# A gated cross-attention and feed-forward kernel: the weighing of values as three fp32r products over the whole array instead of four fp32 column tiles

## The reference

```
q = layernorm(x) @ Wq            # 32 heads of 32
k, v = ctx @ Wk, ctx @ Wv        # 8 key-value heads of 32, each serves 4 query heads
scores = q k^T / sqrt(32)
attn = softmax(scores)
out = attn v                     # per head: 128 queries x 128 keys, by 128 keys x 32
x = x + tanh(g_xattn) * (out @ Wo)
x = x + tanh(g_ffn) * ffn(layernorm(x))
```

## Time and profile before

| | |
|---|---|
| median of 3 runs | 1945.35 us (1944.39 to 1946.03) |
| the profiled execution's own time | 1945.35 us |
| its span, first to last instruction | 1943.6 us |
| mean granted TensorE clock | 0.995 of full speed |
| busy: TensorE, VectorE, ScalarE, GpSimd | 98%, 60%, 45%, 44% of the span |
| matmul instructions of PV | 512, from 67.2 to 627.5 us |

### The profile page before, as it was taken

How to read it: one execution, slowest core, us unless ns; L and a number is a source line. 1 busy time by engine, 2 the same in 40 slices (tenths; PEclk the granted TensorE clock), 3 DMA queues, 4 the chain that set the end, 5 groups by cost and what they waited for, 6 DMA issues and landing times.

```text
span 1943.6 us, 27413 instructions
## 1 busy us (share of the span) xinstructions
PE 1903.7 (98%) x9312; PEld 1555.2 (80%) x9312; DVE 1171.9 (60%) x1622; ACT 884.2 (45%) x2109; POOL 848.1 (44%) x632
## 2 busy tenths in 40 slices
PE   7999999999999999999999999999999999999999
PEld 6768877877876888888888878888888888887887
DVE  7657656755764865555555567765555555545565
ACT  4883793596387343333332344443333333333333
POOL 1330341232133588888888411114675766630000
PEclk9999999999999999999999999999999999999999
DMA  5225226324424235354545866662232333257665
GB/s 207 85 96 198 88 61 219 125 61 167 150 63 182 94 125 200 135 183 156 179 153 183 282 221 237 211 222 98 91 125 81 108 108 108 87 189 249 214 222 186
DMA packets 125948, 298.78 MB, mean 154 GB/s; under 512 B 12704, under 2 KB 21920, under 8 KB 120480
## 3 DMA queue, kind: packets, MB, share of 16 engines
q1 hardware_dynamic: 125568, 297.06, 44.8%
q10 hardware_dynamic: 288, 0.52, 0.1%
HBM read 221.25 MB, written 71.57 MB: 151 GB/s over the span
## 4 chain that ended last, share of the span: by engine, by line
PE 79%; ACT 10%; DVE 3%; DMA 3%; issue 2%; POOL 2%; SPq 0%; POOLq 0%; ACTq 0%; DVEq 0%
PE ps L1593 25%; PE ps L1595 25%; PE ps L1594 25%; ACT pb L918 6%; ACT pt L861 1%; DMA xo<-x1d 1%; PE ps L1653 1%; DMA raw<-ws 1%; ACT qo_l L861 1%; PE ps L1643 1%; PE ps L1689 1%; DVE qo_l L1203 1%; DVE qo_h L1203 1%; PE ps L1809 1%; ACT qo_h L861 1%
## 5 line engine op out<-in xcount | busy, mean ns | idle before, releaser
L1593 PE MATMUL ps<-xop_h,w_h 128*128 128x512 f32 x1208 | 471.8, 391 | 0.0
L1595 PE MATMUL ps<-xop_h,w_l 128*128 128x512 f32 x1208 | 470.1, 389 | 0.0
L1594 PE MATMUL ps<-xop_l,w_h 128*128 128x512 f32 x1208 | 469.9, 389 | 0.0
L1171 DVE TENSOR_TENSOR bl<-raw,bh 128x1024 fp32r<-128x1024 f32 x154 | 197.4, 1289 | 146.6 <-ACT bh L861 146.6
L861 ACT ACTIVATE bh<-raw 128x1024 fp32r<-128x1024 f32 x154 | 163.1, 1061 | 233.8 <-PE ps L1595 212.8
L1595 PEld LDWEIGHTS ps<-xop_h,w_l 128*128 128x128 f32 x1208 | 226.7, 188 | 47.1
L1593 PEld LDWEIGHTS ps<-xop_h,w_h 128*128 128x128 f32 x1208 | 226.8, 188 | 46.6 <-DVE cc L1405 0.3
L1594 PEld LDWEIGHTS ps<-xop_l,w_h 128*128 128x128 f32 x1208 | 226.8, 188 | 46.4
L1593 PE MATMUL ps<-bh 128*128 128x512 f32 x616 | 244.9, 398 | 6.0 <-DVE xo L1496 3.4
L1171 DVE TENSOR_TENSOR w_l<-fraw,w_h 128x512 fp32r<-128x512 f32 x130 | 135.9, 1046 | 185.8 <-ACT w_h L861 185.8
L1595 PE MATMUL ps<-bh,bl 128*128 128x512 f32 x616 | 241.6, 392 | 0.0
(11 more groups left out here) (156 smaller groups left out, 3447.9 us busy)
## 6 DMA issues: line engine op xcount, KB each, us to landing
fraw<-in_wf SPq DMA_DIRECT2D x42, 1024.0 KB, 5.1
raw<-hs SPq DMA_DIRECT2D x154, 256.0 KB, 3.0
hs<-hsum SPq DMA_DIRECT2D x22, 1280.0 KB, 5.7
raw<-ws SPq DMA_DIRECT2D x110, 256.0 KB, 3.9
wc_raw<-in_wc SPq DMA_DIRECT2D x44, 512.0 KB, 4.5
dw<-in_wd SPq DMA_DIRECT2D x11, 1024.0 KB, 7.7
hs<-hb SPq DMA_DIRECT2D x44, 256.0 KB, 2.0
raw<-in_wd SPq DMA_DIRECT2D x44, 256.0 KB, 3.9
```

The lines of the kernel that those rows point to most:

```text
L1171: return nc.vector.tensor_tensor(out, whole, hi.bitcast(F32), ALU.subtract)
L1593: pe.matmul(out, w_hi_, m_h, start=first, stop=False, skip_group_check=goes_on)
L1594: pe.matmul(out, w_hi_, m_l, start=False, stop=False, skip_group_check=goes_on)
L1595: return pe.matmul(out, w_lo_, m_h, start=False, stop=last, skip_group_check=goes_on)
```

## The change

`weigh_values` becomes twelve fp32r matmuls for each pair: `three` for each of the four heads, into the whole 128 partitions of bank 5, summed over the heads (the sum starts at the first head and ends at the last). The weights are 128x128 tiles `vp_h` and `vp_l`, zero but for the 32 columns of the head. For that:

- the transposed probabilities and the values are kept as high and low parts: ScalarE's copies write the high ones, and VectorE gets a subtraction for each unit (`pt_out`) and for each sequence's values (`v_out`);
- GpSimd clears `vp_h`, `vp_l` once a group and copies the values into their places, two copies for each pair (`build_vp`); there are two buffers, so the copies for pair m + 2 wait for PV of pair m (`pv_done`);
- waits for `pt_ready` and `v_ready` on TensorE become waits for the low parts, and PV waits for `vp_built` too.

```diff
-        pt = at("pt", [P, 2, 4, 2 * P], F32, o_x1)
+        pt_h = at("pt_h", [P, 2, 4, 2 * P], F32R, o_x1)
+        pt_l = at("pt_l", [P, 2, 4, 2 * P], F32R, o_x1 + 8192)
...
-        vc = at("vc", [P, NB, 2 * P], F32, o_vc)
+        vc_h = at("vc_h", [P, NB, 2 * P], F32R, o_vc)
+        vc_l = at("vc_l", [P, NB, 2 * P], F32R, o_vc + 4096)
...
+        vp_h = at("vp_h", [P, 2, 4, P], F32R, o_vp)
+        vp_l = at("vp_l", [P, 2, 4, P], F32R, o_vp + 4096)
...
+            def build_vp(m):
+
+                a, b = m // NB // 2, m % NB
+                for vp, vc in ((vp_h, vc_h), (vp_l, vc_l)):
+                    dst = bass.AP(vp, (m % 2) * 4 * P, [[8 * P, P], [P + HD, 4], [1, HD]])
+                    ins = nc.gpsimd.tensor_copy(dst, vc[:, b, a * P:(a + 1) * P].rearrange("p (j d) -> p j d", j=4).bitcast(F32))
+                ins.then_inc(vp_built, 1)
...
+                nc.gpsimd.memset(vp_h[:, :, :, :].bitcast(F32), 0.0)
+                nc.gpsimd.memset(vp_l[:, :, :, :].bitcast(F32), 0.0).then_inc(vp_zero, 1)
+                pool.wait_ge(vp_zero, g + 1)
+                pool.sem_inc(passed, 1)
+                pool.wait_ge(v_lo, g * NB + NB)
+                pool.sem_inc(passed, 1)
+                build_vp(0)
+                build_vp(1)
                 for n in range(UNITS):
...
                     nc.gpsimd.tensor_tensor(p, p, r, ALU.mult).then_inc(normed, 1)
+                    if n >= 5 and n % 2 == 1:
+                        m = (n - 5) // 2
+                        pool.wait_ge(pv_done, g * PAIRS + (m + 1))
+                        pool.sem_inc(passed, 1)
+                        build_vp(m + 2)
...
+            def v_out(G, b):
+                dve.wait_ge(v_hi, G * NB + (b + 1))
+                minus(vc_l[:, b, :], ps[:, b % 2, 2 * P:4 * P], vc_h[:, b, :]).then_inc(v_lo, 1)
...
+            def pt_out(g, n):
+                m, gi = n // 2, n % 2
+                dve.wait_ge(pt_hi, g * UNITS + (n + 1))
+                where = (slice(None), m % 2, slice(None), slice(gi * P, (gi + 1) * P))
+                minus(pt_l[where], ps[:, 3 + n % 2, :].rearrange("p (j q) -> p j q", j=4), pt_h[where]).then_inc(pt_lo, 1)
...
                         o_out(g, m)
+                    if 3 <= n < UNITS + 3:
+                        pt_out(g, n - 3)
...
             def weigh_values(g, m):
-                pe.wait_ge(pt_ready, g * UNITS + (2 * m + 2))
+                pe.wait_ge(pt_lo, g * UNITS + (2 * m + 2))
+                pe.wait_ge(vp_built, g * PAIRS + (m + 1))
                 if m >= 1:
                     pe.wait_ge(o_lo, g * PAIRS + m)
-                k, b = m // NB, m % NB
                 for j in range(4):
-                    head = slice(HD * j, HD * j + HD)
-                    ins = pe.matmul(ps[head, 5, 0:2 * P], vc[:, b, k // 2 * P + HD * j:k // 2 * P + HD * j + HD],
-                                    pt[:, m % 2, j, :], start=True, stop=True, tile_position=(0, HD * j))
+                    ins = three(ps[:, 5, 0:2 * P], vp_h[:, m % 2, j, :], vp_l[:, m % 2, j, :],
+                                pt_h[:, m % 2, j, :], pt_l[:, m % 2, j, :], j == 0, j == 3)
                 ins.then_inc(pv_done, 1)
```

More of the change, by code:

```diff
@@ L236, in gated_cross_attention_ffn @@
         q_hi, q_lo = sem("q_hi"), sem("q_lo")
-        pt_ready = sem("pt_ready")
+        pt_hi, pt_lo = sem("pt_hi"), sem("pt_lo")
         o_hi, o_lo = sem("o_hi"), sem("o_lo")
-        v_ready = sem("v_ready")
+        v_hi, v_lo = sem("v_hi"), sem("v_lo")
         k_hi, k_lo = sem("k_hi"), sem("k_lo")
@@ L255, in gated_cross_attention_ffn @@
         kb_zero = sem("kb_zero")
+        vp_zero = sem("vp_zero")
         kb_first = sem("kb_first")
         kb_in = [sem(f"kb_in{c}") for c in range(2)]
+        vp_built = sem("vp_built")
         maxed = sem("maxed")
@@ L886, in kv_out @@
                 copy(kn[:, b % 2, :], ps[:, b % 2, 0:2 * P]).then_inc(k_nat, 1)
-                copy(vc[:, b, :], ps[:, b % 2, 2 * P:4 * P]).then_inc(v_ready, 1)
+                copy(vc_h[:, b, :], ps[:, b % 2, 2 * P:4 * P]).then_inc(v_hi, 1)
             def kt_out(G, b):
@@ L909, in pt_out @@
                     act.wait_ge(pv_done, g * PAIRS + (m - 1))
-                copy(pt[:, m % 2, :, gi * P:(gi + 1) * P],
-                     ps[:, 3 + n % 2, :].rearrange("p (j q) -> p j q", j=4)).then_inc(pt_ready, 1)
+                copy(pt_h[:, m % 2, :, gi * P:(gi + 1) * P],
+                     ps[:, 3 + n % 2, :].rearrange("p (j q) -> p j q", j=4)).then_inc(pt_hi, 1)
             def exps(g, n):
@@ L1347, in body @@
                     normalise1(G, 3, next_x(3))
+                    v_out(G, 0)
                     split_ct(G, 2)
                     split_wc(G, 0)
+                    v_out(G, 1)
                     split_ct(G, 3)
@@ L1354, in body @@
                     split_wc(G, 1)
+                    v_out(G, 2)
                     k_out(G, 1)
@@ L1357, in body @@
                     xt_out(G, 3)
+                    v_out(G, 3)
                     k_out(G, 2)
@@ L1518, in _ @@
             normalise1(0, 0, x1[:, 0, :])
+            v_out(0, 0)
             normalise1(0, 1, x1[:, 1, :])
@@ L1524, in _ @@
             dve.wait_ge(tg_ready, 1)
+            v_out(0, 1)
             normalise1(0, 3, x1[:, 3, :])
@@ L1528, in _ @@
             xt_out(0, 0)
+            v_out(0, 2)
             k_out(0, 1)
@@ L1534, in _ @@
             split_wc(0, 1)
+            v_out(0, 3)
             k_out(0, 2)
@@ L1625, in scores @@
                 if n == 1:
-                    pe.wait_ge(v_ready, g * NB + NB)
+                    pe.wait_ge(v_lo, g * NB + NB)
                 elif n == 2:
@@ L1665, in kv @@
                 if b >= 2:
-                    pe.wait_ge(v_ready, G * NB + (b - 1))
+                    pe.wait_ge(v_lo, G * NB + (b - 1))
                 for k in ks:
@@ L1694, in body @@
                 pe.wait_ge(xt1_lo, g * 8 + 8)
-                pe.wait_ge(v_ready, g * NB + NB - 1)
+                pe.wait_ge(v_lo, g * NB + NB - 1)
                 q_tile(g, 0, range(K8))
```

2 lines of the change are left out of this document (1 added, 1 removed).

## The result

| | before | after |
|---|---|---|
| median | 1945.69 us (1944.39 to 1946.70, 4 runs) | 1975.36 us (1974.56 to 1978.11, 4 runs) |
| ratio to before, 95% interval | | 1.0155 [1.0138, 1.0173] |
| the profiled execution's own time | 1945.35 us | 1973.73 us |
| its span | 1943.6 us | 1971.4 us |
| mean granted TensorE clock | 0.995 | 0.999 |

The changed kernel is slower by 29.7 us; 1973.6 was predicted, in a range of 1962 to 1988.

The account below looks back on a forecast made before the run. TensorE, busy 98% of the span, was taken as the bound: 1945.35 + 40.7 for longer PVs - 12.4 of waits taken back = 1973.6 us. The forecast was 1967 to 1981 (chance 0.62), the 8-in-10 range 1962 to 1988.

Parts of the forecast that it names:

- The matmuls: TensorE's PV in the attention: twelve matmuls 0.117 us apart add 0.64 or 0.63 us each PV, 40.7 us gross.
- Rival D: PV's old form runs four passes a head one after the other, so the change wins 30 us: 1915 us; chance 0.02.
- What waits give back: TensorE's waits near PV and the transposes take back 3.1 us a group, 12.4 us for four.
- every other PV of the first stage: Odd PVs there lose their 0.30 us wait as TensorE's road gets longer: four a group, 1.2 us back.
- The PV in front of the long wait: Inside the 8.54 us chain from ninth to tenth PV, with its 2.34 us wait: one PV hidden, 0.63 us back.
- The end of the group: From unit 26's transposes to unit 31's, two PVs, 1.28 us, fit in 1.54 us of waits: 1.3 us back.
- VectorE at nothing: VectorE's 128 new subtractions, 87 us in all, add 0 us since row maxima stay in time; bound 22 us.
- GpSimd at nothing: GpSimd's 128 new casts, 0.4 us each, fit in its waits and add 0 us; bound 8 us.
- A: VectorE's subtraction or GpSimd's casts become a wait, nothing is taken back: 1996 us, half of it 1985; chance 0.19.
- B: ScalarE paces the attention loop more than seen, partly hiding TensorE's time; 27.9 us of waits go: 1958 us; chance 0.14.
- C: In steps with a PV, ScalarE sets the round throughout and PV runs in its shadow: 1945 us; chance 0.03.
- The place: TensorE's span grows only in the attention, about 7 us a group; first-stage four-unit round from 11.06 to about 12.0 us.

Follow-up runs that it names:

- the helpers alone: Changed kernel with its new VectorE and GpSimd work and waits, but PV again as four fp32 matmuls in column tiles, high parts only: 1950.22 us, 1.0027 to the kernel before.
- the moved copies: Kernel before, with the copies of transposed probabilities of the odd units from 9 to 31 of each group moved from ScalarE to VectorE: 1937.74 us, 0.9971.
- the order edit: Kernel before, with the query tile's split moved behind the split of the pair's output on ScalarE and VectorE: 1938.48 us, 0.9966.

## Why the prediction was right, point by point

*The matmuls: right.* Forecast 0.64 and 0.63 us a PV, measured 0.67 and 0.64: 10 x 0.67 + 6 x 0.64 = 10.5 us a group, 42 in all for 40.7. The score matmuls of the earlier trace rows were the right like: 0.12 us apart. That PV sums twelve times into one bank costs nothing extra.

*Why it is more at all: right, and shown, but for one reading.* The old form pays 0.57 us for four heads because they lie side by side. Twice of it adds 0.43; over the whole array the same four take 1.54. Rival D, the old form as one pass behind the other, fell with that. The four-passes rule of the Trainium skill (FP8 and Floating Point Precision, TensorE Precision Notes) would make four fp32 passes against three of fp32r 4 to 3 for one head; the experiment gives 0.385 to 0.36, so a pass of the fp32 form took less here (0.096 us) than an fp32r matmul with weights of its own (0.12).
The prediction read the gap in front of the old PV and the longer first score matmul behind it as the price of two changes of the tiling mode. The fp32 matmuls over the whole array change no tiling, and have 0.43 us in front (0.53 in column tiles, 0.35 for fp32r) and 0.31 for the first score matmul (0.22 and 0.12). So only about 0.10 us in front goes with the tiles, and the longer matmul behind stands without a change of tiling too (the weights are wider in that kernel as well, so the shares are rough). The forecast does not change by it, since it took both from rows as one price.

*What waits give back: too high, and made good by luck.* Forecast 3.1 us a group. Where the clock is full in both kernels it is 10.5 - 8.0 = 2.5, 10 us in all, and TensorE's own waits say the same, 18.9 less 8.9. By the table: every other PV of the first stage gave back 0.34 three times, not four, 1.0 for 1.2. The first of them was late instead and cost 0.39 more than its matmuls: the forecast had missed that ScalarE still works off a backlog there, so that VectorE's subtraction is on its path. The PV in front of the long wait was hidden but for 0.09, as forecast, and that wait is 1.41 us (1.7 forecast):

```profile
122.88 0.36 PE L1640 MATMUL ps<-pt_h,vp_h 128*128 128x256 f32 x1 [1.41 <-DVE qo_l L1198]
```

The end of the group, PV 11 to 15, gave back 2.6 - 1.1 = 1.5, for 1.3. The clock did the rest, and I had it nowhere: two groups of before had lost 1 us each to it that those of after don't lose, and the feed-forward part 3 us. In all 42 - 10 is 32 us, 0.8 more come from the first PV's later start (no cause was looked for), 2 + 3 of clock go off, and that is the 27.8 of the span, where 28.3 were forecast. That the profiled execution's 1973.73 us lie at the forecast's 1973.6 is luck: waits gave back 2.4 us less than forecast, and the clock, which the forecast doesn't have, 5.

*VectorE at nothing: nearly.* It was 1 to 2 us here (PV 1 of each group) and 5 us where TensorE's steps are as short as before's. My argument, that the maximum is in time since ScalarE gets its transposes late, holds from 78.74 us on in the first group, and not in the 23 us before, in which ScalarE has work queued all the time. The price of a subtraction is as read, groups by line of the kernel after, 0 to 700 us, with busy time, mean ns and idle time before:

```profile
L1198 DVE TENSOR_TENSOR pt_l<-ps,pt_h 128x512 fp32r<-128x512 f32 x128 | 87.6, 684 | 29.7 <-ACT pt_h L888 29.1
...
L701 POOL CAST vp_h<-vc_h 128x128 fp32r<-128x128 f32 x64 | 31.3, 490 | 11.4 <-PE ps L1642 10.4 <-POOL vp_l L719 1.1
...
L701 POOL CAST vp_l<-vc_l 128x128 fp32r<-128x128 f32 x64 | 21.8, 341 | 0.0
```

*GpSimd at nothing: right.* Its copies take 0.29 us when nothing disturbs them, the mean is 0.49 and 0.34, for the 0.4 I took. Its wait for a PV two back cost it 10.4 us and nobody else anything.

*The rivals.* A (VectorE or GpSimd a wait, 1985 to 1996) needed a wait for `pt_l` or `vp` in the kernel after: there is none. B (ScalarE paces more, 1958) is refuted by ScalarE's idle time, which rose: for the transposes 27.4 us in 37 waits, with 13.9 in 19 before. B's price was also worked out too low: its 27.9 us of waits hold 4.4 + 4.6 of PEld, the loading of weights, beside TensorE's own 18.9, so it would be 1945.35 + 40.7 - 18.9 = 1967. C needed PVs under 0.89 us; they take 1.52.

*The place: right.* 8.0 us a group at full clock and 7.5 in the mean for the forecast 7.1, and the round of four units 12.08 us (2 x 6.04) for 11.08 before and the forecast 12.0.

## What to carry to other kernels

Before small fp32 matmuls are traded for fp32r products, count what they occupy together and not what one of them takes: four in column tiles cost 0.57 us here, and twelve cheaper ones over the whole array 1.52. Waits beside a lengthened stretch take back a part (10 of 42 us here): read the same distance in every group and each turn of a loop, and see which wait is only an order of queues. Make the same mend in both kernels before the two are compared, since a mend in one place can bring up a wait in the next. Where one repeat of a loop is longer than the others, look at the granted clock of that stretch before it is put down to a wait. Extra work on an engine that is 60% busy was free here where its consumer waits for somebody else, and was paid at the start of a group, where the consumer has a backlog.

## What the runs showed of the hardware

*A cast held up beside a subtraction.* GpSimd in order of time, and then VectorE, both in the kernel after:

```profile
118.25 1.29 POOL L701 CAST vp_h<-vc_h 128x128 fp32r<-128x128 f32 x1
119.48 0.29 POOL L701 CAST vp_l<-vc_l 128x128 fp32r<-128x128 f32 x1
```

```profile
117.95 1.43 DVE L1198 TENSOR_TENSOR wr_l<-wr_raw,wr_h 128x1024 fp32r<-128x1024 f32 x1 [0.77 <-ACT wr_h L888]
```

The cast takes 1.29 us for its usual 0.29 and ends about where VectorE's subtraction of two SBUF operands does (119.4). The next one, behind it, is undisturbed. The Trainium skill (SBUF — State Buffer, SBUF: two separate sides) says that the two share a port pair that one of them locks for an instruction; the trace agrees, and it is GpSimd that is held here. No run took the subtraction away, so the lock itself is argued from these rows.

*Column tiles overlap almost fully.* A second set of four fp32 matmuls in column tiles adds 0.43 us to the first's 0.57, and one over the whole array takes 0.385: so four in tiles cost little more than one over the whole array.

*The clock can fall behind a short wait.* In the traces of the kernel before, of the helpers alone, of the same without subtractions, of PV twice, of the moved copies and of the order edit the clock fell once to three times in the attention, each time to 0.50 and behind waits of PV or of the transposes in front of it; in the kernel before it was behind two of four waits of 2.34 us, at about 1 us each. In the traces of the other six kernels it fell there not once. What decides it was not tested.
